# One fused attention and expert kernel: load order, query products, factor scaling and score biases moved

## The reference

```python
# L0_xattn: spectral attention; q from the normalised x, k and v from the context, 8 columns each
corr = real(ifft(fft(q) * conj(fft(k)))).mean(axis=(0, 1))    # 128 lags, one vector for all
W_topk, I_topk = top_k(corr, 11); W_topk = softmax(W_topk)    # v is then rolled and added, times Wout
# L0_ffn: two composed weights, 32 primitives of rank 64
w = softmax(top_k(logits, 32)); W1 = einsum('k,kir,kro->io', w, fc1_A, fc1_B); W2 = same with fc2
h = gelu(layernorm(x) @ W1); x = x + h @ W2
# L1_xattn: softmax(Q K^T / sqrt(D)) V, with biases on Q and K
# L1_ffn: per token the two best of eight experts
probs = softmax(logits); top_p, top_i = top_k(probs, 2); top_p = top_p / sum(top_p)
for _ in range(2): ...   # hidden = gelu(ctx @ w1[expert]); ctrl = hidden @ w2[expert]; update, then refine
```

## Time and profile before

| | |
|---|---|
| median of 3 runs | 336.79 us (336.31 to 337.1) |
| the profiled execution | 337.09 us |
| its span in the trace | 335.3 us |
| PE busy | 315.3 us (94%) |
| DVE busy | 264.6 us (79%) |
| ACT busy | 194.7 us (58%) |
| PE on the chain that ended last | 75% of the span |

### The profile page before, as it was taken

One profiled execution on the slowest core, in us unless ns is written; L12 is line 12 of the kernel. 1 busy time (PEld: TensorE's weight loads), 2 busy tenths in 40 slices (PEclk: granted clock), 3 DMA queues, 4 the chain that ended last, 5 costly groups with the idle time before them and its releaser, 6 DMA issues.

```text
span 335.3 us, 4378 instructions
## 1 busy us (share of the span) xinstructions
PE 315.3 (94%) x1482; PEld 222.4 (66%) x1490; DVE 264.6 (79%) x541; ACT 194.7 (58%) x307; POOL 45.7 (14%) x55
## 2 busy tenths in 40 slices
PE   4989999989999989986989999999999999998995
PEld 4764598555466557664757767777767777766763
DVE  1472847676668997979999889999987996999693
ACT  3410123545869657688887867648367546635733
POOL 0030012112111610239710121001001000000000
PEclk9978999999999999999999999999999999999999
DMA  7999970000000000063170651001001000000001
GB/s 259 428 421 313 269 289 0 0 3 1 0 0 2 0 3 0 0 194 60 63 180 11 188 95 33 0 0 33 0 1 33 1 0 28 5 0 31 2 0 63
DMA packets 13173, 25.21 MB, mean 75 GB/s; under 512 B 608, under 2 KB 9056, under 8 KB 11872
## 3 DMA queue, kind: packets, MB, share of 16 engines
q1 hardware_dynamic: 11712, 20.75, 17.2%
q0 software_dynamic: 1440, 4.19, 6.8%
HBM read 16.55 MB, written 1.05 MB: 52 GB/s over the span
## 4 chain that ended last, share of the span: by engine, by line
PE 75%; DVE 15%; ACT 5%; issue 3%; DMA 1%; DVEq 0%; ACTq 0%
PE ps L1379 71%; PE ps L1479 1%; DVE ring L1041 1%; DVE hm_even L1060 1%; DMA pA<-in_packA 1%; DVE st L828 1%; ACT ring L555 1%; PE ps L1596 1%; ACT L555 1%; DVE a L844 1%; PE ps L1500 1%; PE ps L1466 1%; DVE hm_even L1053 1%; ACT hB L547 1%; DVE ctxT L1270 1%
## 5 line engine op out<-in xcount | busy, mean ns | idle before, releaser
L1379 PE MATMUL ps<-hm_even,ew_hi 128*128 128x512 f32 (+1 forms) x152 | 49.7, 421 | 1.9 <-ACT xi L533 1.2
L1379 PE MATMUL ps<-hm_odd,ew_hi 128*128 128x512 f32 (+1 forms) x148 | 47.6, 421 | 0.0
L1379 PEld LDWEIGHTS ps<-hm_even,ew_hi 128*128 128x128 f32 (+1 forms) x152 | 26.3, 188 | 8.5 <-issue 2.4
L1379 PEld LDWEIGHTS ps<-hm_odd,ew_hi 128*128 128x128 f32 (+1 forms) x148 | 25.7, 189 | 5.5 <-issue 0.5
L607 ACT ACTIVATE hid<-ps,pB 128x512 f32<-128x512 f32 x32 | 21.8, 688 | 11.0 <-PE ps L1379 10.3
L477 POOL TENSOR_TENSOR zz<-zz,mhalf 128x4 f32<-128x4 f32 x12 | 14.8, 1236 | 95.8 <-DVE zz L933 95.8
L1379 PE MATMUL ps<-hm_even,ew_lo 128*128 128x512 f32 (+1 forms) x72 | 25.3, 392 | 0.0
L1379 PE MATMUL ps<-x_hi,w1x_hi 128*128 128x512 f32 x40 | 18.6, 466 | 3.9 <-ACT hid L607 2.0
L1379 PE MATMUL ps<-hm_odd,ew_lo 128*128 128x512 f32 (+1 forms) x64 | 22.3, 394 | 0.0
L1041 DVE SCALAR_TENSOR_TENSOR ring<-ring,pB,hid 128x1024 f32<-128x1024 bf16 x16 | 20.5, 1282 | 0.6
L1379 PE MATMUL ps<-zz,pB 128*128 128x512 f32 (+3 forms) x52 | 19.5, 504 | 0.5 <-DVE zz L1314 0.5
(11 more groups left out here) (323 smaller groups left out, 758.6 us busy)
## 6 DMA issues: line engine op xcount, KB each, us to landing
ring<-in_fc1b SPq DMA_DIRECT2D x4, 1024.0 KB, 17.9
ring<-in_fc2a SPq DMA_DIRECT2D x4, 1024.0 KB, 7.1
hm_odd<-hm_odd SPq DMA_DIRECT2D x4, 512.0 KB, 2.9
packC<-in_packC SPq DMA_DIRECT2D x1, 1152.0 KB, 9.1
pB<-in_packB SPq DMA_DIRECT2D x1, 1077.0 KB, 8.3
ctxT<-in_ctxT SPq DMA_DIRECT2D x2, 512.0 KB, 6.3
xtok<-in_xtok SPq DMA_DIRECT2D x1, 1024.0 KB, 8.9
xT<-in_xT SPq DMA_DIRECT2D x1, 1024.0 KB, 10.9
```

The source lines that it names most:

```text
L1379: return pe.matmul(out, lhsT, rhs, start=start, stop=stop)
```

## The change

Seven things are done.

1. SP issues `a1` and the first quarter of the first weight's second factor ahead of `xtok` and `xT`.
2. DVE makes `wcol` early, and multiplies `a1` in four quarters, each behind one of the last four groups of keys. ACT, not DVE, multiplies `b2`, in 16 instructions of 128 columns, and PE waits for them one by one.
3. The query products stand in pairs behind the second to the ninth product of `W1`; the Fourier products behind the eleventh (before: the fourth), the correlation behind the fifteenth (before: the eighth).
4. The spectral output stands behind the twelfth product of `compose_w2(0)` (before: ahead of it).
5. `scores_bias(0)` to `(2)` stand between the compositions and ffn_up; only `(3)` stays in the loop. ACT's copies move along.
6. In the experts, `second_exp(1, 2)` comes ahead of the Tanh of step 0, and `second_exp(3, 1)` moves from there to ahead of the Tanh of step 1.
7. `weigh(3, 1)` on POOL follows a step later, and `expand_weights(3)` on PE with its copies on ACT moves from step 2 to step 3.

```diff
-                                   (xtok[:, :, :], d_xtok, "in_xtok"), (xT[:, :], d_xT, "in_x"),
-                                   (a1[:, :, :], d_a1, "in_a1")):
+                                   (a1[:, :, :], d_a1, "in_a1"), (b1_piece(0), d_b1[:, 0:KP, :], "in_b1_0"),
+                                   (xtok[:, :, :], d_xtok, "in_xtok"), (xT[:, :], d_xT, "in_x")):
...
                 if s == 1:
                     weigh(1, 2)
+                if s == 2:
                     weigh(3, 1)
...
+            act.wait_ge(sem("wcol"), 4)
+            act.wait_ge(sem("in_b2"), 16)
+            for k in range(KC):
+                act.activation(b2[:, k, :], b2[:, k, :], ACT.Copy, scale=wcol[:, 1, k:k + 1]).then_inc(sem("b2s"), 1)
...
+            second_exp(1, 2)
             squashed(0, GATE)
-            second_exp(1, 2)
-            second_exp(3, 1)
...
                 if s == 2:
                     weights_evac(2, 7, 6)
+                if s == 3:
                     weights_evac(3, 7, 6)
...
                 halt1(s - 1)
+                if s == 1:
+                    second_exp(3, 1)
                 squashed(s, parts(s)[1])
...
+            def scale_a1(i):
+
+                dve.wait_ge(sem("wcol"), 4)
+                dve.wait_ge(sem("in_a1"), 16)
+                k = slice(i * KP, (i + 1) * KP)
+                dve.tensor_tensor(a1[:, k, :], a1[:, k, :], wcol[:, 0, k].unsqueeze(2).to_broadcast([128, KP, D]),
+                                  ALU.mult).then_inc(sem("a1s"), 1)
...
+                if g >= VG - 4:
+                    scale_a1(g - (VG - 4))
...
-            dve.tensor_tensor(a1[:, :, :], a1[:, :, :], wcol[:, 0, :].unsqueeze(2).to_broadcast([128, KC, D]),
-                              ALU.mult).then_inc(sem("a1s"), 1)
...
-            dve.tensor_tensor(b2[:, :, :], b2[:, :, :], wcol[:, 1, :].unsqueeze(2).to_broadcast([128, KC, D]),
-                              ALU.mult).then_inc(sem("b2s"), 1)
...
             pe.wait_ge(sem("k"), NCH)
-            compose_w1(0)
...
+            for k in range(KC):
+                i = k // KP
+                if k % KP == 0:
+                    pe.wait_ge(sem("a1s"), i + 1)
+                    pe.wait_ge(sem(f"in_b1_{i}"), 16)
+                last = mm(bank[6][:, :], a1[:, k, :], b1_piece(i)[:, k % KP, :], start=k == 0, stop=k == KC - 1)
...
+                if 1 <= k <= B // 2:
+                    pe.wait_ge(sem("in_x"), 16)
+                    for b in (2 * k - 2, 2 * k - 1):
+                        last = mm(bank[0][:, b * DH:(b + 1) * DH], xT[:, b * S:(b + 1) * S], A("wq8"))
+                    if b == B - 1:
+                        last.then_inc(sem("q8_ps"), 1)
+                if k == 10:
+                    pe.wait_ge(sem("k8"), 2 * VG)
+                    pe.wait_ge(sem("q8"), 1)
...
-            compose_w2(0)
+            compose_w2(0, {12: spectral_out})
...
             compose_w2(2)
+            scores_bias(0)
             ffn_up(0, (0, 1))
             compose_w2(3)
+            scores_bias(1)
             ffn_up(0, (2, 3))
+            scores_bias(2)
             ln_spread("ffn", 1)
-            scores_bias(0)
...
-                                           2: {3: hidden_rest, 5: weights_2, 6: weights_3}}.get(s, {}))
+                                           2: {3: hidden_rest, 5: weights_2}, 3: {5: weights_3}}.get(s, {}))
```

More of the change, by code:

```diff
@@ L402, in _ @@
                                    (ctxT[:, T // 2:T], d_ctxT[:, T // 2:T], "in_ctx_1"),
-                                   (xtok[:, :, :], d_xtok, "in_xtok"), (xT[:, :], d_xT, "in_x"),
-                                   (a1[:, :, :], d_a1, "in_a1")):
+                                   (a1[:, :, :], d_a1, "in_a1"), (b1_piece(0), d_b1[:, 0:KP, :], "in_b1_0"),
+                                   (xtok[:, :, :], d_xtok, "in_xtok"), (xT[:, :], d_xT, "in_x")):
                 sp.dma_start(dst, src).then_inc(sem(name), 16)
-            for i in range(4):
+            for i in range(1, 4):
                 sp.dma_start(b1_piece(i), d_b1[:, i * KP:(i + 1) * KP, :]).then_inc(sem(f"in_b1_{i}"), 16)
@@ L616, in _ @@
                 .then_inc(sem("w2"), 1)
+            crep_evac(1)
             act.wait_ge(sem("in_B"), 16)
@@ L624, in _ @@
             act.activation(wh2s[:, :], W("wh2"), ACT.Copy).then_inc(sem("wf1_hi"), 1)
-            for c in range(1, NCH):
-                crep_evac(c)
+            crep_evac(3)
             def state_high(s):
@@ L811, in _ @@
             dve.tensor_scalar(cen, ident, -1.0 / D, None, ALU.add).then_inc(sem("wqc"), 1)
+            dve.wait_ge(sem("lge"), 2)
+            link(dve.reciprocal(lg_n[:, 4:6], lg_n[:, 2:4]))
+            for i in range(2):
+                for half in range(2):
+                    p = slice(64 * half, 64 * half + 64)
+                    dve.tensor_scalar(wcol[p, i, :], lg_e[p, i, half:PRIM:2], lg_n[p, 4 + i:5 + i], None,
+                                      ALU.mult).then_inc(sem("wcol"), 1)
             dve.wait_ge(sem("bvo_ps"), 1)
@@ L1412, in _ @@
                 mm(bank[6 + c % 2][:, :], wqk, ctxT[:, ck(c)]).then_inc(sem("k_ps"), 1)
[L1413 to L1424, removed]
@@ L1427, in _ @@
-            pe.wait_ge(sem("a1s"), 1)
-            pe.wait_ge(sem("k"), NCH)
-            compose_w1(0)
[L1430 to L1445, removed]
+            pe.wait_ge(sem("k"), NCH)
+            for k in range(KC):
[4 more added lines that the diff above has]
+                last = mm(bank[6][:, :], a1[:, k, :], b1_piece(i)[:, k % KP, :], start=k == 0, stop=k == KC - 1)
+                if k % KP == KP - 1:
+                    last.then_inc(sem("w1_ps" if k == KC - 1 else "w1_piece"), 1)
+                if 1 <= k <= B // 2:
[7 more added lines that the diff above has]
+                    pe.wait_ge(sem("q8"), 1)
+                    mm(bank[4][0:NF, 0:256], A("cl"), qk[:, :, :])
+                    mm(bank[4][0:NF, 256:512], A("sl"), qk[:, :, :]).then_inc(sem("dft_ps"), 1)
+                if k == 14:
+                    pe.wait_ge(sem("reB"), 2)
+                    mm(bank[5][0:NF, 0:128], reB[:, 0, :], A("cf"), stop=False)
+                    mm(bank[5][0:NF, 0:128], reB[:, 1, :], A("sf"), start=False).then_inc(sem("cor_ps"), 1)
@@ L1446, in compose_w2, with spectral_out @@
+            def spectral_out():
+                pe.wait_ge(sem("abf"), 2)
+                pe.wait_ge(sem("cw"), 1)
+                mm(bank[4][:, 0:128], cw[:, 0, :], ab_f[:, 2, :], stop=False)
+                mm(bank[4][:, 0:128], cw[:, 1, :], ab_f[:, 3, :], start=False).then_inc(sem("y_ps"), 1)
+            def compose_w2(f, between={}):
                 pe.wait_ge(sem(f"in_a2_{f}"), 16)
                 for k in range(KC):
+                    if f == 0:
+                        pe.wait_ge(sem("b2s"), k + 1)
+                    if k in between:
+                        between[k]()
@@ L1680, in _ @@
                 if t == 0:
-                    for c in range(1, NCH):
-                        scores_bias(c)
+                    scores_bias(3)
                 if t + 2 < NCH:
@@ L1812, in refine_a @@
                         pe.wait_ge(sem("cb"), 3 + j)
-                    if s == 1:
-                        pe.wait_ge(sem("cb"), 7 + j)
+                    if s in (1, 2):
+                        pe.wait_ge(sem("cb"), 2 * s + 3 + j)
                     mm(bank[7 - j], wf1_hi[:, w], xn_hi, stop=False)
@@ L1907, in weights_3 @@
                 def weights_3():
-                    pe.wait_ge(sem("cb"), 6)
+                    pe.wait_ge(sem("rr"), 2)
+                    pe.wait_ge(sem("th"), 2)
                     expand_weights(3, 7, 6)
```

6 lines of the change are left out of this document (2 added, 4 removed).

## The result

| | before | after |
|---|---|---|
| median of 20 runs | 336.79 us (336.27 to 337.45) | 338.02 us (336.46 to 339.16) |
| ratio | | 1.0029, 95% interval 1.0017 to 1.0042 |
| the profiled execution, its span | 337.09, 335.3 us | 336.63, 334.5 us |
| PE / DVE / ACT busy | 315.3 / 264.6 / 194.7 us | 311.8 / 262.4 / 202.0 us |

The change made the kernel 0.3% slower; the prediction was 336.1, with 334.6 to 338.0 as its range. One thing is needed to read the number. Every run comes with its span and the mean clock that TensorE was granted. The profiled execution above is of the smaller group. It shows the change as it was costed, and only another trace shows what went wrong in two of three.

The account below looks back on a forecast made before the run. The last chain piece, 120.8 us of PE from 187.97 us on, was taken as the bound, earlier work counting only by when PE gets there. Loading -2.3 and experts +1.55 gave -0.75, so 336.1 us, range 334.6 to 338.0.

Parts of the forecast that it names:

- The clock falls again: Rival, loading: clock falls at the pause before 18.8 or by mixing in 8-column products; 3.3 us more, 339.4; chance 0.1.
- the term of 2.3 us for loading: Loading, composing and score biases: third `ln_spread` at 66.7 instead of 69.03, a lead of 2.3 us up to the experts.
- The loading stretch, step by step: Loading and composing: times from W1's start at 18.8 to the token transposes at 43.9, 1.7 us ahead.
- A pair: Two query products placed behind a W1 product: 0.45 us at 2.4 GHz, from 3.63 / 8.
- DVE's quarters of `a1`: Loading: 0.57 us each, fitting between the last key groups and done by about 15.6.
- ACT's 16 multiplications of `b2`: Loading: 16 x 0.3 us from around 30, ending by 35, before W2 at 37.5, so covered.
- POOL's hold of the third `ln_spread`: After the score biases: POOL's power ends at 66.6, so PE's `ln_spread` comes at 66.7 rather than 65.4.
- DVE's subtractions hold POOL: Ahead of the third `ln_spread`: DVE's weight splits and statistics, to the end of POOL's power, take 5.3 us from DVE's scaling.
- So the slow clock costs 3.3 us: Loading: W1's first four products take 6.72 us at mostly 1.2 GHz, against 3.44 for the next eight rows.
- The experts: Steps 0 to 3: PE 2.2 us late for a Gelu, 1.1 back, 0.75 lost at 187.97, 0.8 more in step 3; 1.55.
- DVE swallowing the gain: Rival "Slower": DVE's splits hold POOL's power and the load's lead falls below 1.3; 337.0 to 338; chance 0.2.

Follow-up runs that it names:

- experiment 8: Experiment 1's kernel with DVE's two weight subtractions ahead of the scaling of chunk 1 instead of behind it: 334.59 us, ratio 0.9940.
- experiment 11: The kernel before, unchanged, profiled a second time: 336.69 us, span 334.9.
- experiment 3: The changed kernel, unchanged, run again with a second profile: 338.26 us median of 12; the profiled execution took 338.70.
- experiment 1: The changed kernel with edits 6 and 7 undone, so the loading part (edits 1 to 5) alone: 335.27 us, ratio 0.9956.
- experiment 2: The kernel before with edits 6 and 7 alone, the experts' part: 339.22 us median of 6, ratio 1.0063.
- experiment 7: The changed kernel with edit 6 undone (Exps both behind the Tanh of step 0) and edit 7 kept: 334.78 us, ratio 0.9944.
- experiment 5: The changed kernel with eight products, results never read, in PE's idle time in step 2: 336.93 us, 11 runs.
- experiment 6: The changed kernel with two products, results never read, in PE's idle time in step 2: 337.17 us, 11 runs.
- experiment 12: Experiment 7's kernel with two more ACT instructions that nothing waits for: 335.28 us, against 334.78.
- experiment 4: The changed kernel with its 16 query products as one block ahead of W1 again: 338.16 us median of 12.
- experiment 9: The changes of experiment 7 and experiment 8 together: 333.82 us, ratio 0.9918.

## Why the prediction was wrong

The step that failed is the rival "The clock falls again": it had a chance of 0.1, two places in the loading stretch, and was left out of the range. The clock fell at a third place, behind the wait for `hid` in step 2 that the prediction had itself computed, in 21 of 32 executions. Beside it the term of 2.3 us for loading was 0.8 too large, and 0.3 us outside the span had no term; these two alone would have left the median near 337, within the range but without the gain.

**The loading stretch, step by step: right in its places.** Predicted and read in the profiled execution: W1 starts 18.8 / 18.65; Fourier 31.9 / 31.77; correlation 36.2 / 36.06; W1 done 37.5 / 37.37; `abf` 41.6 / 41.58 with a wait of 1.4 / 1.37; transposes 43.9 / 43.85; POOL's hold of the third `ln_spread` 66.7 / 66.67. A pair costs less than predicted (0.36 from start to start, 0.45 predicted) and the product beside it more (0.94, 0.86 predicted), 1.30 together as in the sum. DVE's quarters of `a1` took 0.68 each instead of 0.57, and still ended ahead of the last key; ACT's 16 multiplications of `b2` ran from 29.60 for 4.78 us, done before W2. That DVE's subtractions hold POOL was confirmed by experiment 8.

**"So the slow clock costs 3.3 us": mis-sized.** That was one execution, and the 3.3 sets a row's length against a distance from start to start. From start to start the four products and the 3.44 at full clock give 28.91 - 22.35 - 3.44 = 3.1 us of loss, and 28.14 - 22.91 - 3.44 = 1.8 in the second trace of before, so the price of the fall changes by 1.3 us from one execution to the next. The gain up to the experts is 2.36 us between the two traces that began at 14.03, 1.0 between the two that began late (third `ln_spread` 53.67 us behind the keys in experiment 11, 52.64 in experiment 3), and 1.5 between medians (experiment 1). I took the term 2.3 into the sum as if it were fixed; it was 0.8 too large.

**The experts: mechanism right, size near.** Predicted was PE 2.2 late at the third tile of hidden(3), 1.1 back from the moved transposes, 0.8 lost again in step 3, 1.55 in all. Read: 2.1 to 2.2 (2.36 to 0.22), 1.0 back, 0.35 more up to 186.41, 0.8 lost to the end, 1.56 in all. In step 0, where I expected neither gain nor loss, one Exp less lets PE take up the third tile of hidden(2) 2.73 us ahead (150.16 against 152.89), 0.37 more than before it; DVE's routing takes that away again, 2.40 at step 2's first tile. That is against the trace of before. Experiment 1's trace, which began at the same time (14.02), has a span of 333.2, so beside the loading part the experts cost 334.5 - 333.2 = 1.3. For edit 7 the signs of the parts hold as predicted (more back than lost), and alone it gains 0.5. The table load cost what its row said: 165.95 to 167.25 and 168.96 to 170.26 are 1.30 each. The Trainium skill, "ScalarE: Activation LUTs", section "What ACT_TABLE_LOAD costs", has 2.66 us a switch, of which the load alone is 1283 ns; this trace agrees on the load (1.28) and shows no time for the rest.

**The rival "The clock falls again": the step that failed.** Its two places were the pause before 18.8 and the mixture with 8-column products. There the clock held: 1.00 from 0 to 170 us in both traces of the changed kernel. I had computed the place where it fell, PE 2.2 us late for `hid` in step 2, and asked only who is late behind it. That a wait of PE can put the work behind it at 1.2 GHz was in my own reading of the loading stretch, for a wait of 1.0. Experiments 2 and 3 show the fall there, 1 and 7 that step 2 keeps its clock without the split Exps, 5 and 6 that the idle time is its cause. The 21 executions lie 1.2 to 2.6 us above the 336.6 of the others, but not all of that is the fall: it cost 1.3 in the one trace that has it, 0.75 there was the late start.

**The sum as measured.** 336.8 before; 1.5 less by the loading part; 1.3 more by the experts; 0.3 more outside the span; that is 336.9, near the medians of the kernels with fillers (336.93 and 337.17). The group at clock 1.000, at 336.6, is a little faster; the one trace from it started early. The fall then takes the median to 338.0 and 338.3, that is 0.9 to 1.3 more. From the prediction's 336.1 it is 0.8 for the load term, 0.3 outside the span, 0.25 back from the experts, and about 1 for the fall. That the median lies only 0.02 outside the range of 334.6 to 338.0 says nothing for it: the range's upper end was reached by another mechanism, DVE swallowing the gain.

**What stays open.** Why the clock falls in two of three executions and not in all. The start of the keys scatters from 13.93 to 14.77 us over the traces, for a reason that was not followed. No run of the changed kernel stands at 337.1 to 337.5, where a late start without a fall would be, and its two traces have no fall from the early start and a fall from the late one; but experiment 2's trace began early (14.03) and fell in step 2 all the same, so an early start does not prevent it. That all the runs with fillers at 337.1 to 337.5 are late starts is shown by one trace alone.

## What to carry to other kernels

When a step makes the bounding TensorE wait about 2 us, cost two things: the wait, and the chance that what follows runs at 1.2 GHz; a few products into an unused bank removed the loss here (none of 22 runs had it). A stretch of low clock has a different price in each execution, so take its cost from several traces or from medians, and look at the granted clock of every run before comparing medians. And test each part of a bundle alone: without the split Exps (two more table loads for one Exp of 0.2 us) the same bundle gains 2.0 us, and 2.9 with one more swap of order; with them it loses.

## What was not expected of the hardware

- Device time outside the span is 1.8 us for the kernels whose profile counts 307, 309 or 323 ACT instructions, and 2.1 us for those with 325 (the changed kernel, experiments 3 to 6, and experiment 12, made for this). Two instructions that nothing waits for cost 0.3 us outside the span. It was not tried what the step is or where the next one lies.
- TensorE's clock fell behind 16 products of 8 columns (3.63 us "busy") and a wait of 1.0 us in both traces of the kernel before (its mean clock was .984 to .990 in all 23 runs of a session). With the wait, 0.66 us, ahead of the block instead, it fell inside the block in experiment 4's trace, and probably in the five of twelve runs at the same .990.
- Over all traces here PE waited 2.01 to 2.14 us for `hid` between dense products eleven times. 1.2 GHz followed in seven (step 1 in experiments 1, 7, 8, 11 and 12, step 2 in 2 and 3) and not in four (step 1 in the kernel before and experiment 9, step 2 in the changed kernel and experiment 4). Seven such waits of 1.63 to 1.69 us (step 1 in the changed kernel and experiments 2 to 6, step 2 in experiment 6) all left the clock at 1.00.
- In step 1 the same fall is nearly free: experiment 7's run at 1.000 took 334.61 us, its four at .995 334.63 to 334.97, as DVE bounds what follows; the second trace of the kernel before lost 0.4 us of its lead there. A mean clock of .995 says that the clock fell, not that time was lost.
